# Cross attention with an int8 feed forward on one core: row tiles, staging and DMA order of the last batch laid out anew

## What is computed

```python
def attention(Q, K, V, mask, W_q, W_k, W_v, W_o):
    q, k, v = heads(Q @ W_q.T), heads(K @ W_k.T), heads(V @ W_v.T)
    scores = einsum('bhqd,bhkd->bhqk', q, k) / sqrt(32)
    e = where(mask, exp(clip(scores, -50, 50)), 0)
    return merge(einsum('bhqk,bhkd->bhqd', e / sum(e), v)) @ W_o.T

def ffn(lhs, rhs):                      # int8 by row and by column
    s_l, s_r = absmax(lhs, row) / 127, absmax(rhs, column) / 127
    return (round(lhs / s_l) @ round(rhs / s_r)) * s_l * s_r

x = x + attention(layernorm(x), ctx, ctx, mask, W_q, W_k, W_v, W_o)
x = x + ffn(layernorm(x), rhs)
```

## Time and profile before

| | us |
|---|---|
| median of 3 runs | 1775.99 (1774.2 to 1778.95) |
| the profiled execution | 1776.13 |
| its span, first to last instruction | 1774.3 |
| PE busy | 1691.6 (95%) |
| DVE busy | 1465.3 (83%) |
| ACT busy | 1313.7 (74%) |
| POOL busy | 143.1 (8%) |
| stages: attention of batch 0, from | 136 |
| attention of batch 3 (final segments), from | 1349 |
| the last denominators read (after that only the last four row tiles) | 1741.4 |

### The profile page before, as it was taken

One profiled execution on the slowest core, in us unless ns is written; L12 is line 12 of the kernel. 1 busy time (PEld: TensorE's weight loads), 2 busy tenths in 40 slices (PEclk: granted clock), 3 DMA queues, 4 the chain that ended last, 5 costly groups with the idle time before them and its releaser, 6 DMA issues.

```text
span 1774.3 us, 29849 instructions
## 1 busy us (share of the span) xinstructions
PE 1691.6 (95%) x10427; PEld 1008.3 (57%) x10456; DVE 1465.3 (83%) x1692; ACT 1313.7 (74%) x1729; POOL 143.1 (8%) x76
## 2 busy tenths in 40 slices
PE   7999999999999999999999999999998988988987
PEld 7895655555565665656565666666654433443433
DVE  5647888888888989898997989899885878787786
ACT  4557877878777787778787787878776767777774
POOL 0000000000101111010111101011100101010101
PEclk9999999999999999999999999999999999999998
DMA  7786555566665665667566566757657796769832
GB/s 256 221 237 166 150 146 137 149 149 166 158 171 142 162 174 136 188 162 207 128 158 166 141 187 161 206 126 179 167 143 202 187 201 143 170 149 219 185 96 78
DMA packets 233284, 295.91 MB, mean 167 GB/s; under 512 B 28200, under 2 KB 138792, under 8 KB 232616
## 3 DMA queue, kind: packets, MB, share of 16 engines
q1 hardware_dynamic: 230968, 289.21, 63.3%
q10 hardware_dynamic: 2160, 4.72, 1.0%
HBM read 201.59 MB, written 92.00 MB: 165 GB/s over the span
## 4 chain that ended last, share of the span: by engine, by line
PE 77%; DVE 8%; issue 5%; ACT 5%; DMA 3%; SPq 1%; POOL 0%; ACTq 0%; POOLq 0%; DVEq 0%
PE tile L921 24%; PE wsum L958 22%; PE scores L943 21%; DVE acc L1482 4%; ACT probs L1188 4%; PE scores L921 2%; PE scores L1081 2%; PE tile L975 2%; DMA den_c<-denoms 1%; DMA v_parts<-v_stage 1%; PE tile L1081 1%; PE tile L983 1%; PE tile L1044 1%; PE tile L1021 1%; DMA o_parts<-sums 1%
## 5 line engine op out<-in xcount | busy, mean ns | idle before, releaser
L1188 ACT ACTIVATE probs<-scores 128x1024 f32<-128x1024 f32 x939 | 914.0, 1027 | 238.2 <-PE scores L943 177.5
L1482 DVE TENSOR_TENSOR acc<-acc,probs 128x2048 f32<-128x2048 f32 x428 | 977.9, 2285 | 77.4 <-ACT probs L1188 65.4
L958 PE MATMUL wsum<-probs,v_sb 128*32 128x512 f32 x4096 | 501.0, 607 | 0.0
L943 PE MATMUL scores<-q_stack,k_stack 128*128 128x512 f32 x1536 | 446.2, 410 | 10.4 <-ACT probs L1188 9.6
L943 PEld LDWEIGHTS scores<-q_stack,k_stack 128*128 128x128 f32 x1536 | 265.8, 188 | 225.8 <-ACT probs L1188 131.7
L958 PEld LDWEIGHTS wsum<-probs,v_sb 128*32 128x32 f32 x4096 | 108.9, 110 | 249.8 <-issue 231.9
L1572 POOL TENSOR_TENSOR rstd<-var_eps,minus_half 128x1 f32<-128x1 f32 x48 | 103.9, 2164 | 1205.1 <-DVE var_eps L1381 1205.1
L1482 DVE TENSOR_TENSOR acc<-probs 128x2048 f32<-128x2048 f32 x32 | 73.3, 2292 | 78.9 <-PE tile L975 45.0
L1081 PE MATMUL scores<-q_stack,k_stack 128*128 128x512 f32 x342 | 111.5, 428 | 18.0 <-ACT probs L1188 18.0
L921 PE MATMUL tile<-ctx_hi,wk_hi 128*128 128x256 f32 x412 | 117.1, 284 | 4.6 <-DVE ctx_lo L1391 4.6
L921 PE MATMUL tile<-ctx_hi,wk_lo 128*128 128x256 f32 x412 | 116.6, 283 | 0.0
(11 more groups left out here) (236 smaller groups left out, 1992.0 us busy)
## 6 DMA issues: line engine op xcount, KB each, us to landing
k_stack<-k_parts SPq DMA_DIRECT2D x312, 256.0 KB, 7.4
q_stack<-q_parts SPq DMA_DIRECT2D x124, 256.0 KB, 6.7
v_sb<-v_parts SPq DMA_DIRECT2D x80, 256.0 KB, 7.5
v_parts<-v_stage SPq DMA_DIRECT2D x64, 256.0 KB, 4.8
raw<-ctxT SPq DMA_DIRECT2D x27, 512.0 KB, 6.3
k_parts<-stage_hi SPq DMA_DIRECT2D x96, 128.0 KB, 4.5
k_parts<-stage_lo SPq DMA_DIRECT2D x96, 128.0 KB, 2.5
x_in<-x SPq DMA_DIRECT2D x33, 256.0 KB, 4.2
```

Of the source, the lines that this page charges most:

```text
L943: last = nc.tensor.matmul(scores[:, h, :], k_stack[:, kt // 4, h, (kt % 4) * P:(kt % 4 + 1) * P], q_stack[:, qb, h, :], start=True, stop=True)
L958: last = nc.tensor.matmul(wsum[DH * h:DH * h + DH, :], v_sb[:, kt, DH * h:DH * h + DH], probs[:, n % RING, h, :], start=(kt == 0), stop=(k ...
L1188: nc.scalar.activation(probs[:, slot % RING, 2 * pair:2 * pair + 2, :], score_banks(seg, slot, pair), ACT.Exp, scale=1.0 / math.sqrt(DH)). ...
L1482: nc.vector.tensor_tensor(acc[:, :, :], other, probs[:, slot % RING, :, :], ALU.add).then_inc(sems["add_done"], 1)
```

## The change

In the last batch the events of the twelve row tiles get a table by tile (ROW_PAIRS, pairs 0 to 63 over the four segments), with the addition of the result as an event of its own, and each engine visits one event per tile and pair in a changed place; the order in which O, T, F and the denominators use their bank is worked out from the table (D_BEFORE) and each waits for the user before it. DIRECT is (15,) instead of (14, 15) and holds for the final segments only. The high and low part of a half's result get buffers of their own in the final segments (the unused w_hi["k"] and w_lo["k"]); ACT copies the next sums once attn_split is reached. Denominators are multiplied behind the sums, and sums are copied ahead of denoms. The product moves from step 8 to step 6 of a half, the den_c DMA from step 2 to step 1. SP's other steps are put in another order. In the first batch three events move (FIRST_BATCH). In the last segment of a batch the context split is done ahead of the last exponential and addition.

```diff
+FIRST_BATCH = {**BOTH, 4: [("K", 0, 3)], 6: [], 7: [("V", 0, 0, 0)], 12: [], 13: [("load_x", 1), ("V", 0, 1, 2), ("split", 1)], 14: [("X", 0)]}
-DIRECT = (14, 15)
+DIRECT = (15,)
-ROW_TILES = 3
-PAIRS = {"O": (1, 3, 10), "norm": (2, 4, 11), "quant": (3, 5, 12), "whole": (4, 6, 13), "T": (5, 7, 14), "F": (6, 9, 15)}
+ROW_TILES = 12
+ROW_EVENTS = ("O", "norm", "quant", "whole", "T", "F", "add")
+ROW_PAIRS = (
+    (3, 3, 6, 7, 9, 11, 12), (7, 8, 9, 11, 16, 17, 18), (15, 15, 16, 17, 20, 21, 22),
+    (19, 19, 22, 23, 25, 27, 28), (23, 24, 25, 27, 32, 33, 34), (31, 31, 32, 33, 36, 37, 38),
+    (35, 35, 38, 39, 41, 43, 44), (39, 40, 41, 43, 48, 49, 50), (45, 46, 48, 49, 50, 51, 52),
+    (52, 52, 53, 54, 55, 56, 56), (54, 54, 57, 57, 58, 59, 60), (57, 57, 58, 59, 60, 62, 62),
+)
+def order_of_the_bank():
+    users = []
+    for pair in range(G * KT):
+        users += [(event, ROWS_AT[event][pair]) for event in "OTF" if pair in ROWS_AT[event]]
+        if pair % (KT // 2) == 0:
+            users.append(("denoms", pair // (KT // 2)))
+    users.append(("denoms", 2 * G))
+    return dict(zip(users[1:], users))
-        self.direct = DIRECT if self.final or self.last_a else ()
+        self.direct = DIRECT if self.final else ()
+        def o_split(seg, k):
+            return (w_hi["k"][:, k, :], w_lo["k"][:, k, :]) if seg.final else (denoms[:, :].bitcast(F32R), sums[:, :])
...
@@ chain, on SP
-                    if slot == first + 2:
+                    if slot == first + (1 if seg.final else 2):
                         ct.wait_alone(sp, "denoms_copied", k)
                         sp.dma_start(den_c[:, :], denoms[0:P:DH, :])
@@ final_steps, on SP: step and what is issued (waits as before)
-   q: 1   k, last quarter: 2   v, last quarter: 3   next k: 5, 9, 13   next v: 7, 11, 14
+   q: 8   k, last quarter: 5   v, last quarter: 3   next k: 6, 10, 13  next v: 7, 11, 14
-   rows of o_parts: slot 16 of segments 0, 2, 3 and slot 31 of segment 3
+   rows of o_parts: slot 18 of segments 0, 2, 3, slot 2 of segments 1, 3, slot 31 of segments 2, 3, in smaller parts
+                    for n in range(FULL - 1):
+                        if STEPS * c + slot == 2 * ROW_PAIRS[n][-1] + 2:
+                            store_rows(sp, n)
+                            if n + 2 < FULL:
+                                load_x_rows(sp, n + 2)
@@ PE, final segments
                         final_rows(even // 2)
+                        sums_of(even - 2)
+                        sums_of(even - 1)
                         if even % KT == 0:
                             denoms_of(even - 2)
-                        sums_of(even - 2)
-                        sums_of(even - 1)
@@ half_done, on ACT
-                    ct.wait(act, "o_stored", 32 * (k - 1))
+                    if seg.final and (k or not seg.before.a):
+                        ct.wait(act, "attn_split", k - 1)
+                    else:
+                        ct.wait(act, "o_stored", 32 * (k - 1))
@@ ACT, pair of steps
                         exponentials(even)
                         for p in seg.pieces(even) + seg.pieces(even + 1):
                             evacuate(p)
-                        exponentials(even + 1)
+                        ends = seg.a and seg.part == G - 1 and even == STEPS - 2
+                        if ends:
+                            for p in seg.at(even + 1):
+                                work(p)
                         n = row_tile(seg, even // 2, "whole")
...
+                        exponentials(even + 1)
@@ DVE, product and low part
-                        if on and even == first + 8:
+                        if on and even == first + (6 if seg.final else 8):
@@ DVE, final segments: order within a pair
-   add(even), norm, scale (F), quant, add(even + 1), add rows, reciprocal, product / low
+   quant, add(even), add rows of an earlier tile, norm, scale (F), add(even + 1), reciprocal, product, low
@@ DVE, other segments
+                        ends = seg.part == G - 1 and even == STEPS - 2
-                                    if (p[0] in SOON) == soon:
+                                    if (p[0] in SOON or ends and p[0] == "split") == soon:
```

More of the change, by code:

```diff
@@ L475, in row_tile @@
         def row_tile(seg, pair, event):
-            if seg.final and pair in PAIRS[event]:
-                return ROW_TILES * seg.part + PAIRS[event].index(pair)
-            return None
+            return ROWS_AT[event].get(KT * seg.part + pair) if seg.final else None
         def score_banks(seg, slot, pair):
@@ L976, in denoms_of @@
                     last.then_inc(sems["acc_summed" if direct else "denoms_full"], 1)
-                    if not direct:
-                        return
-                    for m in (n, n + 1):
+                    for m in direct:
                         ct.wait(pe, "exp_done", 2 * m + 2)
@@ L982, in denoms_of, with bank_free @@
                         for h in range(G):
-                            last = nc.tensor.matmul(dsum[DH * h:DH * h + DH, :], ones[:, :], probs[:, m % RING, h, :], start=False, stop=(m == n + 1))
-                    last.then_inc(sems["denoms_full"], 1)
+                            last = nc.tensor.matmul(dsum[DH * h:DH * h + DH, :], ones[:, :], probs[:, m % RING, h, :], start=False, stop=(m == direct[-1]))
+                    if direct:
+                        last.then_inc(sems["denoms_full"], 1)
+                def bank_free(user):
+                    kind, n = D_BEFORE.get(user, ("", 0))
+                    if kind == "denoms":
+                        ct.wait(pe, "denoms_copied", n - 2 * seg.part)
+                    elif kind:
+                        pe.wait_ge(fs[{"O": "x1_done", "T": "qT_copied", "F": "y_scaled"}[kind]], n + 1)
+                    elif seg.final:
+                        freed(last_d[0])
                 def piece(slot, p):
@@ L1132, in body @@
                         ending = even % KT == 0
-                        direct = (seg if even else seg.before).direct
-                        if ending and direct:
+                        if ending and not seg.b:
                             denoms_of(even - 2)
@@ L1137, in body @@
                         sums_of(even - 1)
-                        if ending and not direct:
+                        if ending and seg.b:
                             denoms_of(even - 2)
@@ L1498, in normalise, with low @@
                             nc.vector.tensor_tensor(sums[:, :], sums[:, :], denoms[:, :], ALU.mult).then_inc(sems["attn_normed"], 1)
+                def low(even):
+                    for first, k, on in ((0, 0, seg.prev and seg.b), (KT, 1, seg.b)):
                         if on and even == first + 12:
                             ct.wait(dve, "attn_hi", k)
-                            nc.vector.tensor_tensor(sums[:, :], sums[:, :], o_hi.bitcast(F32), ALU.subtract).then_inc(sems["attn_split"], 1)
+                            o_hi, o_lo = o_split(seg, k)
+                            if seg.final:
+                                ct.wait(dve, "o_stored", 32 * (k - 2))
+                            nc.vector.tensor_tensor(o_lo, sums[:, :], o_hi.bitcast(F32), ALU.subtract).then_inc(sems["attn_split"], 1)
                 if seg.final:
@@ L1520, in body @@
                             quantise(dve, link_rows, n)
-                        add(even + 1)
+                        add(even)
+                        n = row_tile(seg, pair, "add")
+                        if n is not None and n != row_tile(seg, pair, "F"):
+                            add_rows(dve, nc.vector.tensor_tensor, n)
+                        n = row_tile(seg, pair, "norm")
+                        if n is not None:
+                            residual(dve, link_rows, n, dsum)
                         n = row_tile(seg, pair, "F")
                         if n is not None:
-                            add_rows(dve, nc.vector.tensor_tensor, n)
+                            scale_rows(dve, n, dsum)
+                            if row_tile(seg, pair, "add") == n:
+                                add_rows(dve, nc.vector.tensor_tensor, n)
+                        add(even + 1)
                         invert(even)
-                        normalise(even)
+                        product(even)
+                        low(even)
                     return
```

119 lines of the change are left out of this document (50 added, 69 removed).

## The result

The changed kernel takes 1798.14 us (median of 4, 1794.97 to 1802.24) against 1775.38 for the kernel before: ratio 1.0129, 95% interval 1.0112 to 1.0147. It is slower by 23 us where 46 us less were forecast.

The account below looks back on a forecast made before the run. In the last batch no engine is full; they wait for each other, PE needing 347.7 of 386.8 us. Forecast: 1776.1 - 37 (last batch) - 3 (segment before) - 3.5 (first batch) - 3 (context split) = 1729.6, said as 1730; range 1719 to 1756.

Parts of the forecast that it names:

- PE's need of 341 us and what it allows: Last batch: PE's own work sums to 340.8 us, so the 386.8 us stage can't go below 341; 350 expected.
- DVE keeps up with 14 additions: Last batch: with 14 additions a half for 13, DVE needs 339.5 us, as long as PE's chain.
- Rival 1: Last batch: DVE becomes the bound; only 15 to 28 of 37 us come, total 1740 to 1755; chance 0.24.
- Rival 3: Last batch: ACT's rounding waits for DVE's quantising and stops the exponentials; 1771, or no change at 1775; chance 0.08.
- den_c: Last batch: fetched at step 1, ahead of row and q loads, it removes 13.4 us of DVE's waits.
- x for tile n + 2: Last batch: loaded after tile n's last addition, landing in 4 to 7 us; DVE waits 1 to 3 us twice.
- the 9 us: Last batch: the 2.5% taken as still lost above the 341 us floor, giving 350 us.
- SP's order: Last batch: every load moves; q goes from step 1 to 8, still 8 steps or 22 us before use.
- The product at step 6: Last batch: 9.4 us cover two DMAs, mean 8.2, worst 14.0; no stall in five halves, 1.5 us in three.
- rival 2: Last batch: the product's wait replaces den_c's, DVE standing 4.6 us eight times; 1789; chance 0.08 with its like.
- The last segment before the last batch: Its direct matmuls go, 3.4 us off PE, and DVE gets four additions; gain 3 us, ends 0 and 3.4.
- The context split: Two batch borders: done ahead of the last additions, it removes 2.28 us waits for ctx_lo; gain 3 us.

Follow-up runs that it names:

- e1: The changed kernel with three x buffers instead of two, the third in raw: 1743.1 us, ratio 0.9816 to the kernel before.
- e6: e1 with DIRECT at (14, 15) again in the final segments: 1738.4 us, ratio 0.9791 to the kernel before.
- e10: The kernel before with only the den_c DMA moved to step 1 of a half in the final segments: 1764.6 us, ratio 0.9946.
- e7: e1 with SP's q load back at step 1 and the last k quarter at step 2: 1777.6 us, ratio 1.0029 to the kernel before.
- e4: The changed kernel with x of tiles 2 to 11 issued from ACT's queue, one pair after the addition: 1747.4 us, ratio 0.9843 to the kernel before.
- e8: The kernel before with only the moved first-batch pieces (FIRST_BATCH), run once: six halves of that batch took 294.1 us for 292.0 before.
- e2: The changed kernel with SP's q load back at step 1 and the last k quarter at step 2: 1822.0 us, ratio 1.0252 to the kernel before.

## Why the prediction was wrong

*PE's need of 341 us and what it allows.* Right. With x out of the way (e1) the first six halves are 42.1 to 44.2 us at a clock of 1.00, for the 43 to 44.5 named. The stretch that the prediction put at 350 us, from the first copy of the denominators to the last denominators read, takes 352.6 in e1 and 350.1 in e6 (386.8 before, 412.3 in the changed kernel).

*DVE keeps up with 14 additions.* Right but for the last half of e1, where PE waits 5.25 us. Rival 1 is out by its own signs, DVE busy over 0.97 with halves of 45 to 47: in e1 DVE is busy 317.6 of 352.6 us and six halves are shorter. That e1's 1743 us lies in the range of rival 1 has another cause, given below. Rival 3 is out: in the changed kernel ACT's rounding waited 8.2 us for DVE in all.

*den_c.* Right: 13.4 us of waits to 1.2, and worth 6 to 13 us alone (e10). That it brings the store of the reciprocals nearer to q and k wasn't seen.

*x for tile n + 2: this is the step that failed.* The prediction took "a landing of 4 to 7" for x and one pair between addition and use at tiles 3 and 6 only, so DVE would wait 1 to 3 us twice, and left that in the 9 us. The landing fits the medians over the whole kernel before (4.2 for x_in, 5.7 for xr). In the last batch of that kernel the very same loads took 7.9 and 8.5 us in the median and up to 10.8; nobody waited for them there, so no list of waits showed it. And the change made it 13.3 and 16.4, by placing 2 MB of k, then 1 MB of q and 1 MB of k, around x in the same queue. With 16 us plus the wait until SP gets to it x needs some four pairs (17.5 us) ahead of its use. By ROW_PAIRS all ten tiles loaded in this way have one to three (one pair at tile 11 also, which the prediction passed over), and DVE waited in nine of the ten. Its size: 64.1 us of DVE's time for the 2 to 6 forecast. Taking these waits away (e1) gave 55 us of the kernel's time.

*SP's order.* "q from step 1 to 8, still 8 steps or 22 us before its use" was right for q: only two weight loads of PE waited for q, 0.8 us each. It asked only whether the moved load comes in time, not what comes behind it. Each moved load was priced by its own user.

*The product at step 6.* A reading under it was wrong: 2.2, 3.8 and 6.8 us are the landing of the 8 KB store, not of the load, as the earlier trace rows and the prediction have it. The list of DMA issues of the kernel before, from 1354 to 1740, gives the 3.8 to the store and no landing to the load:

```profile
denoms<-recip_row SPq DMA_DIRECT2D x8, 256.0 KB
recip_row<-recip_c SPq DMA_DIRECT2D x8, 8.0 KB, 3.8
```

So the 8.2 and 14.0 us count the store twice, no run shows the load's own leg, and rival 2's 4.6 us a half rest on it too. The prediction put 4.5 us on the product in all. In the changed kernel SP waits for the store 10.7 us in eight, 1.3 each, and DVE waits for denoms 0.2 us in all: the cost was nothing, because q and k had been moved behind it. Rival 2 is the right mechanism at the wrong place: it comes up as soon as q and k go first (e7: 43.6 us, 34 us of time). The two moves of the change belong together, which the prediction didn't see.

By the Trainium skill's fit ("DMA: Bandwidth & Descriptors", Anatomy of one DMA), made for the other way of issuing, a load of 256 KB is estimated at 2.0 + 0.6 = 2.6 us. Here the same 256 KB of x take from 2.6 us (e4) to 18.3 (the changed kernel): for these loads the fit is the lower end, and what stands ahead in the queue sets most of the rest.

*The other parts.* The last segment before the last batch: from its first copy of the denominators to the first scores of the next 1345.8 - 1251.1 = 94.7 us for 96.1, which is 1.4 of the 3 forecast; the other direct step falls after that point. It is 94.7 in all nine kernels with this edit, 96.1 to 96.8 in the three without. The context split: the waits of 2.28 us at both borders are gone. From one segment's copy to the one two halves on, 585.00 - 482.01 = 103.0 us for 105.8 at the first border, a gain of 2.8, but 996.60 - 890.18 = 106.4 for 105.6 at the second, where PE now waits 1.81 us for the rows' DMA. The nine kernels with the edit took 102.7 to 104.1 and 104.8 to 106.4 there, the three without 103.6 to 105.8 and 105.6 to 106.5: between the means it is 1.5 and 0.6 us, 2 of the 3 forecast, with little certainty. The first batch: 3.5 forecast, nothing found; the 6.4 us of PE's waits were read right, that they would go was argued from two empty pairs and was not so.

*In sum.* Without the late x the forecast was 1730 and the kernel takes 1743 (e1) or 1738 (e6). Of the 8 to 13 us missing almost nothing is in the last batch. Its stretch takes 352.6 and 350.1 us for 350; in e1 what is over lies in the last two halves, the seventh with events of four tiles (49.9 us) and the last with the wait of 5.25. What is missing lies ahead of it: 9.5 us were forecast from the three parts there, which would put the first copy of the denominators at 1345.1. In the nine kernels that are the same up to that point it is at 1349.5 to 1358.0, with 1351.4 in the middle, for 1354.6 before (1353.3 and 1355.5 in e10 and e8). So these parts brought about 3 us, and the profiled executions of e1 (1356.4) and e6 (1358.0) are late ones, by 5 and 7 us against the middle. Why one and the same piece of program varies by 8 us there is open.

## What to carry to other kernels

Moving a load in a queue has two prices: whether it still comes in time, and what it does to all that is issued after it, in bytes ahead of them. Price a load whose buffer is freed late by its landing in that very stretch, from the view of its tensor, also where nobody waits for it yet. If an in-order engine uses it, another buffer (here 2 KB a partition for 55 us) or a queue of its own (e4, 51 us) makes it safe; the one other order that was tried, e2, only moved the wait.

## What the runs showed of the hardware

The same 256 KB load landed in 2.6 to 18.3 us, depending on what stood ahead of it in its queue. Counted over the loads of x that SP issued in the last batch of all twelve traces (after 1390 us): with four earlier DMAs of SP, most of 256 KB or more, not yet landed, 4.2 to 6.6 us; with twelve or thirteen, 15.7 to 19.0. From a second queue, with as many of SP's under way and the engines as full (share 1.07), it took 9.1 to 9.5 us. An 8 KB store, for the reciprocals, landed in 1.5 us in the median of the changed kernel and in 9.6 with 2 MB ahead of it (e2).
